# Gate products of a gated cross-attention layer: x turned by DMA transposes of 16-bit integers instead of by TensorE

## The reference

```
x = x + tanh(g_xattn) * attention(layernorm(x), ctx, ctx)
h = act_qdq(layernorm(x))
up = act_qdq(h @ lpbq_dequant(w_up).T)
gate = act_qdq(h @ lpbq_dequant(w_gate).T)
sig = fixed_qdq_u16(sigmoid(gate))
gate = act_qdq(gate * sig)
o = act_qdq(gate * up)
x = x + tanh(g_ffn) * (o @ lpbq_dequant(w_down).T)

def act_qdq(x):
    qmax = 32767
    scale = max(max(abs(x)) / qmax, 1e-12)
    return clip(round(x / scale), -qmax - 1, qmax) * scale
```

## Time and profile before

| | |
|---|---|
| median of 3 runs | 1763.51 us |
| profiled execution, its own time | 1763.79 us |
| its span | 1761.5 us |
| granted TensorE clock, mean | 0.983 |
| PE / DVE / ACT / POOL busy | 96% / 76% / 66% / 28% of the span |
| DMA | 173.49 MB, mean 98 GB/s |

### The profile page before, as it was taken

The page is one execution under the profiler, slowest core; times in us unless marked ns, Lnnn a source line. Parts: engine busy times, 40 slices in busy tenths (PEclk is TensorE's granted clock), DMA queues, the critical chain, the costliest instruction groups (busy, mean ns, idle before and its releaser), DMA issues. The chain is left out here.

```text
span 1761.5 us, 36266 instructions
## 1 busy us (share of the span) xinstructions
PE 1690.0 (96%) x12148; PEld 1437.4 (82%) x12148; DVE 1332.0 (76%) x2255; ACT 1163.1 (66%) x3061; POOL 491.1 (28%) x365
## 2 busy tenths in 40 slices
PE   8999999999999999999999999989997999896998
PEld 6788888888888888888888888778885877775998
DVE  6767768677686676767767768876787999898885
ACT  5656666566666665666656666556765999796665
POOL 2322313323232232232322313320001766560000
PEclk9999999999999999999999999998998999897999
DMA  3210001100010010100110000015775886564664
GB/s 131 73 39 26 24 25 36 37 25 36 13 49 24 25 36 22 40 24 25 36 37 25 24 25 36 13 61 201 277 286 187 285 310 231 208 246 167 212 216 145
DMA packets 59998, 173.49 MB, mean 98 GB/s; under 512 B 4528, under 2 KB 34352, under 8 KB 57008
## 3 DMA queue, kind: packets, MB, share of 16 engines
q1 hardware_dynamic: 59952, 172.90, 28.2%
HBM read 96.86 MB, written 76.02 MB: 98 GB/s over the span
## 5 line engine op out<-in xcount | busy, mean ns | idle before, releaser
L377 POOL TENSOR_TENSOR prob<-prob,rsums 128x512 f32<-128x512 f32 x254 | 266.3, 1048 | 813.7 <-DVE rsums L571 667.2
L419 ACT ACTIVATE prob<-masked,neg_max 128x128 f32<-128x128 f32 x1024 | 396.3, 391 | 61.7 <-DVE neg_max L551 61.3
L419 ACT ACTIVATION_READ_ACCUMULATOR prob<-masked,neg_max 128x1 f32 x1024 | 194.3, 190 | 0.0
L567 DVE COPY probT<-trans 128x512 f32<-128x512 f32 x126 | 86.9, 690 | 130.4 <-PE trans L779 127.5
L551 DVE TENSOR_REDUCE neg_max<-masked 128x4 f32<-128x512 f32 x254 | 174.3, 686 | 8.8
L549 DVE TENSOR_TENSOR masked<-score,mask_add 128x512 f32<-128x512 f32 x254 | 172.8, 680 | 0.8
L779 PE MATMUL trans<-ident,prob 128*128 128x128 f32 x1024 | 160.6, 279 | 0.8 <-POOL prob L397 0.8
L428 ACT ACTIVATE probT<-trans 128x512 f32<-128x512 f32 x126 | 75.5, 599 | 119.0 <-PE trans L779 119.0
L434 ACT ACTIVATE qT<-proj 128x512 f32<-128x512 f32 x128 | 76.7, 599 | 111.1 <-PE proj L744 111.1
L804 PE MATMUL score<-kT,qT 64*128 64x128 f32 x2048 | 148.8, 285 | 0.0
L817 PE MATMUL y<-wo_hi,o_hi 128*128 128x256 f32 x508 | 145.9, 287 | 1.8 <-DVE wo_lo L499 1.8
(11 more groups left out here) (249 smaller groups left out, 4617.8 us busy)
## 6 DMA issues: line engine op xcount, KB each, us to landing
gate<-gate_d SPq DMA_DIRECT2D x30, 768.0 KB, 4.8
n_x<-n_x_d SPq DMA_DIRECT2D x25, 512.0 KB, 4.9
gate_d<-stage SPq DMA_DIRECT2D x8, 1536.0 KB, 6.1
n_u_d<-w_raw SPq DMA_DIRECT2D x16, 768.0 KB, 4.0
stage<-n_u_d SPq DMA_DIRECT2D x16, 768.0 KB, 6.0
gate_d<-gate SPq DMA_DIRECT2D x7, 1536.0 KB, 6.1
x_in<-in_x SPq DMA_DIRECT2D x16, 512.0 KB, 3.9
ctx_in<-in_ctx SPq DMA_DIRECT2D x16, 512.0 KB, 3.6
```

The lines of the kernel that those rows point to most:

```text
L377: gp.tensor_tensor(pr, pr, rsums[:, h, :].rearrange("p (b o) -> p b o", o=1).broadcast_to([P, NB, P]), ALU.mult).then_inc(normed, 1)
L419: nc.scalar.activation(prob[:, c % 2, h, b, :], masked[:, h, b, :], ACT.Exp, bias=neg_max[:, h, b:b + 1], accum_out=psums[:, h, b:b + 1]). ...
L567: nc.vector.tensor_copy(probT[:, 1], trans[:]).then_inc(probT_copied[1], 1)
```

## The change

From group 2 on x is no longer turned by PE. ACT quantises the tokens as they come, in `xin`, into `n_tok`, 16-bit, tokens on partitions (`quantise_tokens`, two groups ahead of the products). SP then issues one DMA transposition of the group from `n_tok` to `n_turn` (`turn`), 128 by 1024 elements of 16 bits as eight blocks of 128x128, also two groups ahead. DVE splits `n_turn` instead of `n_full`, with a pattern that puts the blocks (batch, then half of the features) into the order of `n_x` (half of the features, then batch). Groups 0 and 1 go the way they went. A buffer of `xin` is free when its tokens are quantised, so loads are issued four groups ahead of the products instead of two. SP's loop is written out for all 16 groups.

```diff
--- before.py
+++ after.py
@@ -953,6 +953,8 @@
         a2 = sb("a2", [1, 1])
         inv_x = sb("inv_x", [P, 1])
         n_full = sb("n_full", [P, KC, T], I16)
+        n_tok = sb("n_tok", [P, 2, NB * D], I16)
+        n_turn = sb("n_turn", [P, 2, NB * KC, P], I16)
         ring = [st.enter_context(nc.psum_tensor(f"ring{n}", [P, T], F32)) for n in range(RING)]
         tr = hand.banks
 
@@ -965,6 +967,8 @@
         amax_all = sem("amax_all")
         scale_step = sem("scale_step")
         x_int = sem("x_int")
+        tok_int = sem("tok_int")
+        x_turned = [sem(f"x_turned{b}") for b in range(2)]
         first_split = sem("first_split")
         first_ready = sem("first_ready")
         x_split = sem("x_split")
@@ -991,10 +995,29 @@
             def load(t, b):
                 sp.dma_start(xin[:, b], xn2_d[:, t]).then_inc(x_loaded[b], 16)
 
-            def step(t, b, more):
-                if more:
+            def free(t):
+
+                if t < 2:
                     sp.wait_ge(x_transposed, KC * (t + 1))
-                    load(t + 2, b)
+                else:
+                    sp.wait_ge(tok_int, t - 1)
+
+            def turn(t, b):
+
+                sp.wait_ge(tok_int, t - 1)
+                if t >= 4:
+                    sp.wait_ge(x_split, 2 * (t - 1))
+                sp.dma_start_transpose(out=n_turn[:, b], in_=n_tok[:, b]).then_inc(x_turned[b], 16)
+
+            def step(t, b):
+                if t == 0:
+                    free(1)
+                    load(3, 1)
+                if t + 2 < G:
+                    turn(t + 2, b)
+                if t + 4 < G:
+                    free(t + 2)
+                    load(t + 4, b)
                 last = isinstance(t, int) and t == G - 1
                 sp.wait_ge(x_split, 2 * (t + 1))
 
@@ -1006,11 +1029,10 @@
 
             sp.wait_ge(hand.x1_stored, 16 * G)
             sp.wait_ge(hand.xn2_stored, 16 * G)
-            with sp.Fori(0, G // 2 - 1) as i:
-                for b in range(2):
-                    step(2 * i + b, b, True)
-            for b in range(2):
-                step(G - 2 + b, b, False)
+            free(0)
+            load(2, 0)
+            for t in range(G):
+                step(t, t % 2)
             for b in range(2):
                 sp.wait_ge(stored[b], 8 * G - 16 * b)
                 sp.wait_ge(n_x_stored[b], 8 * G)
@@ -1029,6 +1051,12 @@
                     act.wait_ge(x_transposed, KC * t + k + 1)
                     nc.scalar.activation(n_full[:, k, :], tr[k][:], ACT.Copy, scale=inv_x[:, 0:1]).then_inc(x_int, 1)
 
+            def quantise_tokens(t, b):
+
+                act.wait_ge(x_loaded[b], 8 * (t - b) + 16)
+                wait(act, x_turned[b], 8 * (t - 2 - b))
+                nc.scalar.activation(n_tok[:, b], xin[:, b].rearrange("p e d -> p (e d)"), ACT.Copy, scale=inv_x[:, 0:1]).then_inc(tok_int, 1)
+
             def widen_x(t, b, part):
 
                 wait(act, product_done, IC * (t - 1))
@@ -1036,8 +1064,10 @@
                 nc.scalar.activation(xT[b][part][:], n_x[:, b, part], ACT.Copy).then_inc(x_ready, 1)
 
             def step(t, b, last):
-                if not last:
-                    quantise_x(t + 1)
+                if not isinstance(t, int) or t < G - 2:
+                    quantise_tokens(t + 2, b)
+                if isinstance(t, int) and t == 0:
+                    quantise_x(1)
                 for n in range(IC):
                     act.wait_ge(product_done, IC * t + n + 1)
                     if n == 0:
@@ -1077,11 +1107,20 @@
 
             def split_x(t, b):
 
-                dve.wait_ge(x_int, KC * (t + 1))
+                second = isinstance(t, int) and t == 1
+                if second:
+                    dve.wait_ge(x_int, 2 * KC)
+                else:
+                    dve.wait_ge(x_turned[b], 8 * (t - b))
                 wait(dve, n_x_stored[b], 8 * (t - b))
                 wait(dve, x_ready, 2 * (t - 1))
-                v.tensor_scalar(n_x[:, b, 0], n_full[:], -LOW, None, ALU.bitwise_and).then_inc(x_split, 1)
-                v.tensor_scalar(n_x[:, b, 1], n_full[:], LOW - 1, None, ALU.bitwise_and).then_inc(x_split, 1)
+                for part, bits in enumerate((-LOW, LOW - 1)):
+                    if second:
+                        to, of = n_x[:, b, part], n_full[:]
+                    else:
+                        to = n_x[:, b, part].rearrange("p k (e q) -> p k e q", q=P)
+                        of = n_turn[:, b].rearrange("p (e k) q -> p k e q", k=KC)
+                    v.tensor_scalar(to, of, bits, None, ALU.bitwise_and).then_inc(x_split, 1)
 
             def extremes(t, b, h):
 
@@ -1129,8 +1168,6 @@
 
             def step(t, b, last):
                 first = isinstance(t, int) and t == 0
-                if not last and not first:
-                    transpose_x(t + 1, 1 - b)
                 if not first:
                     pe.wait_ge(x_ready, 2 * (t + 1))
                 for n in range(IC):
```

## The result

The changed kernel takes **1753.36 us** (median of 5 runs, 1750.35 to 1756.05), the kernel before 1763.51 (5 runs, 1763.26 to 1765.22): ratio 0.994, 95% interval 0.9924 to 0.9955. It is 10.2 us faster, 0.6%: clear of the noise, but small. The forecast said 7.9, and the time lies 2.2 us under the 1755.6 given and inside the range. In a second set, 6 runs beside 11 of the kernel before, it was 1754.57 against 1764.3, 9.7 us and 0.9947 (0.9931 to 0.9963). The profiled execution took 1751.59 us, its span 1749.3, 12.2 less than the span of before.

A forecast was written before the change was run, and what follows sets the result against it. PE was taken to bound the gate-product stage at 9.28 us per group; the change lowers this to the DVE-ACT loop's 8.84. Gain 7.9: 1763.8 − 7.9 = 1755.9, less 0.3, gives 1755.6 us; range 1750.5 to 1776.

The forecast's parts named there:

- The loop: Gate-product stage, DVE and ACT: split to extremes 2.18 us plus two halves of 3.33, a period of 8.84 us.
- PE's 0.88 us per group: Gate-product stage, PE: cost of a group's transposes; 14 groups give 12.3 us if PE stays the bound.
- The split: DVE's split of x, reading runs of 128: 0.42 us as now, at worst 0.73 us more per group.
- rival 2: DVE's splits lose their speed: 0.73 us more in the loop, period 9.57, kernel 1765.1 us; chance 0.08.
- The tokens: ACT's quantisation of 1024 elements from SBUF: 1.05 us, bounds 0.69 and 1.38, costing nothing.
- The cover: ACT's waiting for PE at the bank evictions, 14.9 us over 36 evictions, read as hiding the token quantisation.
- The DMA term: DMA queue, gate-product stage: 7.34 us per period for other traffic plus 1.2 for the transposition, 8.54, under 8.84.
- Rival 3: DMA becomes the bound from a 1.5 us transposition on; up to 1776 us; chance 0.15 slower, 0.09 in its middle.
- Rival 4: SP or DMA queue: transposition runs as many small ones; eight blocks at 2.6 us give 2008 us; chance 0.11.
- Rival 1: Gate-product stage: PE stays the bound, the loop being shorter than read; 1751.1 us; chance 0.04.
- PE's own bound: Lower end of the forecast range, 1750.5 us, with PE alone setting the pace.
- Everything behind stands as it was: Stages after the gate products: no change in time, so the gain stays 7.9 us.

The follow-up runs named there:

- experiment 1: Changed kernel with ACT's two widenings of x moved behind banks 2 and 3 instead of 1 and 2: 1751.21 us, in a second set 1749.83 us.
- experiment 3: Kernel before without PE's transposes from group 2 on; widening of x in its old place 1751.67 us, one bank later (new place) 1751.99 us.
- experiment 4: Changed kernel with a second DMA transposition of each group from 2 on, into a buffer that nobody reads: 1766.48 us.

## Why the prediction was right

**The loop** was the step that carried the forecast, and it held in each part: from split to extremes 2.12 us (forecast 2.18), the four reductions 6.65 (6.66), period 8.77 (8.84). Group 2's split came at 1209.61 (1209.67), group 3's at 1218.34 (1218.4), group 15's at 1323.66 (1324.5), the last half at 1336.05 (1336.8). The last half is 0.75 us earlier than forecast, about the 12 × 0.07 by which the periods are shorter; of the 0.35 us that attention ended earlier only 0.06 was left at group 2. The stage is 8.3 us shorter (8.4 in the second profiles) against 7.9. Reading PE's 0.88 us per group as the gain (12.3 us in all) would have been too much by half in the stage; experiments 1 and 3 show where the rest of it lay.

**The split** kept its speed (0.42 us, rival 2 dead) although it reads runs of 128. **The tokens** took 1.17 us, forecast 1.05, and cost nothing that shows, as costed: ACT still waits for the split, 2.3 us on average over 13 groups. The cover that the prediction read for it in the earlier trace rows was 14.1 us of waiting for PE and not 14.9, which changes nothing.

**The DMA term** was too large as a sum: 7.34 for the rest, from the busy share, and 1.2 for a transposition make 8.54, which would have made the DMA the bound at 8.40, and experiment 1 shows that it was none. As busy time the 7.34 is right: without any transposition (experiment 3, new place) the queue's share is 88.6% of 8.40, 7.4 us. The step that failed is to take it for what the rest needs; a busy share times the time is not the time that the same bytes need when they are wanted sooner. If the engines set experiment 4's period, the rest needs at most 6.96 and a transposition at least 1.44, so both terms were off, against each other; how the sum splits stays open without that. Rival 3's rule, a bound from 1.5 us on, rested on the same 7.34. The share forecast was 0.93, the profile has 0.988. None of this reached the forecast, since the loop's 8.84 was the larger, but the margin of 0.3 us was thinner than what the terms were known to, and that it held was in part luck.

**Rival 4** (issue or landing tile by tile): the issue holds SP for 2.09 us of 8.77, under the 7 us named as its sign, and eight blocks land in 5.9 us, not in 20.8. **Rival 1** (1751.1, PE the bound) did not come by itself; it came with experiment 1. The range calls 1750.5 PE's own bound, where rival 1 works out 1751.1; nothing hangs on it.

**"Everything behind stands as it was"** is the step that was off in size, by some 1.4 us: the place of an instruction fetch moved. The prediction had no term for it. With it, 8.3 + 1.4 = 9.7 us, what the second set of runs measured. The 10.2 of the first is no different from that: its interval reaches from 7.9 to 13.4 us.

## What to carry to other kernels

When the busy engine is relieved, trace the next cycle through the queues (which instruction stands ahead of the eviction that someone waits for) and take the longer of the two periods as the gain's limit; then look whether one place in a queue buys the rest, as the widening did here for 4.4 us. Judge a DMA bound by what waits for landings or for an issue, not by a share near 1, and give a transposition by DMA the lead that its landing needs before asking what it costs.

## What was not expected of the hardware

- Turning 128×1024 16-bit values by DMA holds SP for 2.09 us (1.35 to 2.22; 2.1 to 6.0 in the stretch with two per group), against 0.47 for a copy of the same bytes, and adds seven to ten points of busy share to what the copy has.
- A DMA share of 0.90 went with a period of 8.40 (a copy), 0.99 with 8.77, 1.00 with 8.40 and 1.04 with 9.84: the share alone tells no bound.
- In the four profiles with one instruction packet of 0.02 MB among 2.3 MB of loads the last of them lands 7.8 to 7.9 us after its issue, in the nine without after 6.3 to 6.6; 36 transposes more on PE, some 260 us earlier, brought the packet back.
- The first 10 us of one and the same stage ran at a granted clock of 0.50 in some executions and 0.7 in others, which is 1.4 us of the stage.
